# A graph-attention layer and a mixture-of-experts layer in one kernel: three reorderings, at the start and at the join of the two layers

## The chip, the cores and the metric

The kernel runs on one core of a Trainium2 chip. The metric is the device time of one execution in microseconds (us). A core has a tensor engine (PE in the profile, its weight loads PEld), a vector engine (DVE), a scalar engine (ACT), GpSimd (POOL) and a sync engine (SP) that here only issues DMAs. Each engine runs its own list of instructions in order and waits on semaphores for the others.

## The reference, cut to what matters

```python
x = x + gnn(layernorm(x), adj, W, a1, a2)      # x: 1354 x 512, adj: 1354 x 1354
#   h = input @ W; f1 = h @ a1; f2 = h @ a2
#   e = leaky_relu(f1 + f2.T, 0.2); attention = softmax(where(adj > 0, e, -9e15), axis=1)
#   gnn = relu(attention @ h)
x = x + ffn(layernorm(x))                       # 8 experts, 512 -> 512 -> 512
#   logits = x @ Wr + br; each token goes to its one best expert, with its softmax weight as gate
#   pos = rank of the token within its expert; tokens with pos >= 1354 // 8 = 169 are dropped
#   expert input = gate * x; hidden = relu(in @ W1 + b1); out = gate * (hidden @ W2 + b2)
```

Everything is float32. Ranks start at 1, so an expert takes up to 168 tokens (CAP).

## The kernel before, in words

Tokens lie in 11 tiles (NT) of 128 rows; the last, tile 10, has 74. There is no planner: the order of each engine's work is written out by hand, as calls one after the other, and semaphores say what each waits for.

**The start.** SP and ACT issue the loads: half of tile 0 of x each, then W in four chunks on ACT's queue, and on SP's queue a1, tile 1 of x, a2, and, once the first chunk of W is there, tiles 2 to 10 and adj. PE first runs five matmuls on constants (spin). Then it spreads a1 over the partitions (spread_a(0), L1373), turns tile 0 (x_turn(0), L1390: four transposes), spreads a2, and multiplies tile 0 by the left half of W (h_raw(0, 0), L1403). Tile 1 follows: x_turn(1), h_raw(1, 0), x_turn(2), then the right halves h_raw(0, 1) and h_raw(1, 1), which need W @ a1 and W @ a2 as two more columns. Those columns come from DVE's dots (L863), four instructions for each of a1 and a2, which need what spread_a left in a bank. The layer norm of a tile is split: DVE takes bn_stats and bn_aggr (stats, L811 and L816), POOL makes rstd and shift (power, L397 to L402), and ACT applies them (normal, L509); tile 0 alone is normalised by DVE (L825). ACT also copies the turned tile out of its bank (x_high, L518) and rounds the parts of W (w_high, L550). From tile 2 on the products are split in high and low parts (h_product, L1421). All the f2 sums meet in f2_turn (L1449).

**Attention.** For each tile scores, softmax, transposes of the probabilities (p_turn, L1469) and their product with h (attend, L1488; attend_last, L1502, for tile 10, in two halves of 256 columns).

**The join.** Tiles 0 to 7 are routed early: the rows of expert 0 among them are gathered by row number (gather_early) into x1_g[0], as 128 rows (j = 0) and 40 rows (j = 1). prepare_first on DVE normalises them and multiplies by the gate into xg0 (L1135); turn_first on PE transposes xg0 (L1609) into the banks of gx0_ps, the input of expert 0. c = 2 and 3 of it use a bank that holds tile 10's attention output until ACT has read it (s_rl 2). Rows of tiles 8 to 10 that go to expert 0 are added there by late_first (L1621), a matmul of the normalised tile with a matrix place_e0 that holds the gate at the row's place (places_first, L1085; place_last, L1096). Tile 10 takes this way: relu_last on ACT (L667, two halves), residual_last on DVE (L971), stats2 (L977), variance2, POOL's power2 (L433) and shift (L454), normal_last on ACT (L674); and beside it x2_turn on PE (L1514), x2_copy on ACT (L658), logits on PE (L1525), then biased, choose, gates and place_last on DVE. first_layer_first (L1740) is expert 0's first product. The rows of the other experts are gathered by POOL (L458) once all rows of x1 are stored. Experts 1 to 7 follow, bound to PE's order.

The names and lines that the change touches: load_x in SP's list, x_high(1) and w_high(1) in ACT's, dots and stats(1) in DVE's; and at the join prepare_first, residual_last, gates (split in zsums and inverses), ranks(1), turn_first with the spins around x2_turn(NT - 1, 0), and the wait of normal_last.

Of the kernel before, what the change touches and what calls it, by code (L numbers as in the profile page):

```python
# [37 lines left out]
def gat_moe(nc, x, adj, W, a1, a2, Wr, br, W1, b1, W2, b2, out):  # L38
# [29 lines left out]
    with ExitStack() as ctx:  # L68
# [208 lines left out]
        def _(sp):  # L277
            def load_x(t):
                R = rows(t)
                w = D if t else H0  # L280
                sp.dma_start(x_all[0:R, t, 0:w], x[t * P:t * P + R, 0:w]).then_inc(s_x[t], 16)

            load_x(0)
            for a, i in ((a1, 0), (a2, 1)):
                sp.wait_ge(s_zero, i + 1)
                sp.dma_start(a_rows[0:1, i, :], a.rearrange("n o -> o n")).then_inc(s_a[i], 16)
                if i == 0:
                    load_x(1)
            sp.wait_ge(s_w[0], 16)
# [207 lines left out]
        def _(act):  # L497
# [74 lines left out]
            w_high(0)  # L572
            normal(1)
            w_high(1)
            x_high(1)
            normal(2)
# [83 lines left out]
            def relu_last():  # L660
# [4 lines left out]
                for j, (done, n) in enumerate(((s_o, NT), (s_ohi, 1))):  # L665
                    act.wait_ge(done, n)
                    act.activation(relu_s[0:R, j * H0:(j + 1) * H0], o_ps[j][0:R, 0:H0], ACT.Relu,  # L667
                                   scale=rinv[0:R, (NT - 1) % 2, :]).then_inc(s_rl, 1)

            def normal_last():  # L670

                R = rows(NT - 1)
                act.wait_ge(s_sh2, 1)
                act.activation(xn2[NT - 1 - EARLY][0:R, :], x_all[0:R, NT - 1, 0:D], ACT.Identity,  # L674
                               scale=x_all[0:R, NT - 1, D + 1:D + 2], bias=shift[0:R, NT - 1:NT]).then_inc(s_xn2, 1)
# [50 lines left out]
            exp_below(1)  # L726
            relu_last()
            x2_copy(NT - 1, 0)
            normal_last()
# [77 lines left out]
        def _(dve):  # L807
# [69 lines left out]
            normal_first()  # L877
            dots(0, 0, 2)
            stats(1)
            dots(0, 2, KC)  # L880
            stats(2)
# [83 lines left out]

            def residual_last():
                t, R = NT - 1, rows(NT - 1)
                for j in range(2):
                    c = slice(j * H0, (j + 1) * H0)
                    dve.wait_ge(s_rl, j + 1)  # L970
                    ins = dve.tensor_tensor(x_all[0:R, t, c], x_all[0:R, t, c], relu_s[0:R, c], ALU.add)  # L971
                ins.then_inc(s_x1, 1)

# [55 lines left out]

            def gates(b):  # L1030


                t0, t1 = BATCH[b]
                dve.wait_ge(s_expl, b + 1)
                dve.tensor_reduce(zsum[:, t0:t1], expl[:, t0:t1, :], AX.X, ALU.add).then_inc(s_zsum, 1)
                dve.wait_ge(s_zsum, b + 1)
                dve.reciprocal(gate[:, t0:t1], zsum[:, t0:t1]).then_inc(s_gate, 1)
# [88 lines left out]
            def prepare_first():  # L1126


                dve.wait_ge(s_x1g[0], 32)
                dve.wait_ge(s_gate0, 1)  # L1130
                dve.tensor_tensor(scale_s[:, 0, :], x1_g[0][:, :, D + 1], gate0[:, :],
                                  ALU.mult).then_inc(s_scale, 1)
                dve.wait_ge(s_scale, 1)
                for j in range(2):
                    dve.tensor_scalar(xg0[0:S[j], j, :], x1_g[0][0:S[j], j, 0:D], x1_g[0][0:S[j], j, D:D + 1],  # L1135
                                      scale_s[0:S[j], 0, j:j + 1], ALU.subtract, ALU.mult).then_inc(s_xg, 1)

# [33 lines left out]
            for t in range(1, NT - 1):  # L1171
# [22 lines left out]
                if t == 2:  # L1194
                    biased(0)
            gates(0)
            token_and_gate(0)
# [11 lines left out]
            prepare_first()  # L1209
            residual_last()  # L1210
            stats2(NT - 1, 0)
            variance2(NT - 1, 0)
            gates(1)
            ranks(1)
            places_first(1, NT - 3)
            places_first(1, NT - 2)
            biased(NT - 1)
            choose(2)
            gates(2)
            place_last()  # L1220
# [75 lines left out]
            def final_first():  # L1296


                dve.wait_ge(s_x1g[0], 64)
                for j in range(2):  # L1300
                    dve.wait_ge(s_y, j + 1)
                    dve.wait_ge(s_xg, j + 1)
                    v = x1_g[0][0:S[j], j, 0:D]
                    dve.scalar_tensor_tensor(v, y_ps[j][0:S[j], :], gate_s[0:S[j], j, 0:1], v, ALU.mult, ALU.add
                                             ).then_inc(s_fin, 1)
# [51 lines left out]
        def _(pe):  # L1357
# [241 lines left out]

            def turn_first(c0, c1):  # L1600


                pe.wait_ge(s_xg, 2)
                for j in range(2):
                    for c in range(c0, c1):
                        if j == 0 and c == 2:
                            pe.wait_ge(s_rl, 2)
                        o = (c % 2) * CAP
                        pe.matmul(gx0_ps[c // 2][:, o + j * P:o + j * P + S[j]],  # L1609
                                  xg0[0:S[j], j, c * P:(c + 1) * P], ident[0:S[j], 0:S[j]],  # L1610
                                  start=(c % 2 == 0 and j == 0), stop=False, is_transpose=True)

# [89 lines left out]
            positions(2, True)  # L1702
            turn_first(0, KC)
            spin(2, slots_ps)
            x2_turn(NT - 1, 0)
            spin(2, slots_ps)
            logits(NT - 1, 0)
# [168 lines left out]
```

## Time and profile before

| | us |
|---|---|
| median of 3 runs | 259.79 |
| the runs | 258.88, 259.79, 261.66 |
| profiled execution, its own time | 260.57 |
| its span | 258.8 |
| PE busy | 247.0 (95%) |
| DVE busy | 188.4 (73%) |
| ACT busy | 133.8 (52%) |
| POOL busy | 88.7 (34%) |

The span runs from the first to the last instruction of the profiled execution; 1.77 us of its own time lie around it. PE is busy nearly throughout, so time can only be saved where PE waits or is slow.

### The profile page before, as it was taken

How to read it: one execution, taken by the hardware profiler on the slowest of the kernel's cores; microseconds unless marked ns; L12 is line 12 of the kernel's file. 1: busy time of each engine (PE TensorE's matmuls, PEld its weight loads, DVE VectorE, ACT ScalarE, POOL GpSimd, SP SyncE). 2: the span in 40 equal slices, each digit the busy share in tenths (PEclk: the TensorE clock that was granted, in tenths of full speed). 3: DMA queues.
4: the chain of work that ended last, by engine and by line, in shares of the span. 5: the costliest groups of instructions: out<-in, count | busy, mean ns of one | idle time of the engine just before them, and what ended most of it. 6: DMA issues, size and time to landing. Idle time of an engine off the chain costs nothing.

```text
span 258.8 us, 4589 instructions
## 1 busy us (share of the span) xinstructions
PE 247.0 (95%) x1625; PEld 208.9 (81%) x1625; DVE 188.4 (73%) x451; ACT 133.8 (52%) x289; POOL 88.7 (34%) x114
## 2 busy tenths in 40 slices
PE   6799999999999899999999999999999999999990
PEld 1489999988788687787787889899978879879780
DVE  3967849997899989888973563866476974974941
ACT  2735785884756765766672320342365364463330
POOL 4324783000024413441330224108462355321522
PEclk9979999999999999999999999999999999999997
DMA  6991000023347779841212204044988798887101
GB/s 223 354 305 42 1 4 1 7 103 107 107 150 174 250 298 276 232 153 62 81 41 84 82 0 137 12 155 131 344 296 264 247 324 294 267 297 248 49 7 44
DMA packets 19210, 40.47 MB, mean 156 GB/s; under 512 B 2810, under 2 KB 3130, under 8 KB 19188
## 3 DMA queue, kind: packets, MB, share of 16 engines
q1 hardware_dynamic: 16196, 34.17, 40.6%
q0 software_dynamic: 2176, 4.80, 5.5%
q10 hardware_dynamic: 816, 1.21, 1.3%
q8 instruction: 13, 0.21, 0.4%
q14 instruction: 9, 0.07, 0.1%
HBM read 32.93 MB, written 8.31 MB: 159 GB/s over the span
## 4 chain that ended last, share of the span: by engine, by line
PE 77%; DVE 9%; ACT 4%; issue 4%; POOL 3%; DMA 1%; POOLq 1%; ACTq 0%
PE bank L1488 21%; PE bank L1754 12%; PE bank L1792 7%; PE bank L1421 6%; PE bank L1820 5%; PE bank L1469 4%; PE bank L1502 3%; PE bank L1403 3%; PE bank L1740 2%; PE bank L1767 2%; DVE adj_s L918 2%; PE bank L1514 1%; PE bank L1621 1%; DVE adj_s L940 1%; PE bank L1525 1%
## 5 line engine op out<-in xcount | busy, mean ns | idle before, releaser
L1488 PE MATMUL bank<-h_hi,pt_hi 128*128 128x512 f32 (+1 forms) x110 | 43.2, 393 | 0.0
L1488 PE MATMUL bank<-h_hi,pt_lo 128*128 128x512 f32 x100 | 41.8, 418 | 0.0
L1488 PE MATMUL bank<-h_lo,pt_hi 128*128 128x512 f32 x100 | 39.1, 391 | 0.0
L428 POOL TENSOR_TENSOR x_all<-x_all,w_raw 128x512 f32<-128x512 f32 x10 | 21.3, 2127 | 50.4 <-ACT w_raw L617 46.7
L1754 PE MATMUL bank<-prob,w 128*128 128x168 f32 x224 | 33.2, 306 | 0.1
L1754 PEld LDWEIGHTS bank<-prob,w 128*128 128x128 f32 x224 | 32.6, 189 | 0.9 <-issue 0.3
L789 ACT ACTIVATE adj_s<-bank,b_cols 128x168 f32<-128x168 f32 x28 | 11.2, 402 | 33.3 <-PE bank L1754 33.3
L1488 PEld LDWEIGHTS bank<-h_hi,pt_hi 128*128 128x128 f32 (+1 forms) x110 | 20.6, 188 | 4.7
L640 ACT ACTIVATE wide<-adj_s,off_b 128x1354 f32<-128x1354 f32 (+1 forms) x11 | 15.7, 1430 | 12.3 <-DVE off_b L933 12.2
L1488 PEld LDWEIGHTS bank<-h_lo,pt_hi 128*128 128x128 f32 x100 | 18.9, 189 | 3.1
L1488 PEld LDWEIGHTS bank<-h_hi,pt_lo 128*128 128x128 f32 x100 | 18.8, 188 | 3.0
L433 POOL TENSOR_TENSOR x_all<-ve,half 128x1 f32<-128x1 f32 (+1 forms) x11 | 6.1, 553 | 42.5 <-DVE ve L984 42.5
L465 POOL DMA_INDIRECT out_dram<-x_all,first x10 | 12.1, 1208 | 23.6 <-DVE x_all L1325 16.6
L940 DVE SCALAR_TENSOR_TENSOR adj_s<-adj_s,off_a,wide 128x1354 f32<-128x1354 f32 (+1 forms) x11 | 17.9, 1629 | 1.3 <-ACT wide L640 1.0
L955 DVE TENSOR_TENSOR pt_lo<-bank,pt_hi 128x512 fp32r<-128x512 f32 (+1 forms) x22 | 14.6, 666 | 5.1 <-ACT pt_hi L628 4.7
L1278 DVE TENSOR_TENSOR h_lo<-adj_s,h_hi 128x256 fp32r<-128x256 f32 x14 | 5.9, 424 | 16.9 <-ACT h_hi L790 16.8
L1469 PE MATMUL bank<-ident,prob 128*128 128x128 f32 (+3 forms) x121 | 18.0, 274 | 0.0
L628 ACT ACTIVATE pt_hi<-bank 128x512 fp32r<-128x512 f32 (+1 forms) x22 | 12.6, 579 | 10.4 <-PE bank L1469 10.4
L918 DVE CUSTOM_DVE_ANT_0 adj_s<-adj_s,wide 128x1354 f32<-128x1354 f32 (+1 forms) x11 | 17.2, 1568 | 0.8 <-ACT wide L569 0.6
L1269 DVE TENSOR_TENSOR h_lo<-w,h_hi 128x1024 fp32r<-128x1024 f32 x14 | 16.5, 1220 | 0.1
L458 POOL DMA_INDIRECT x_all<-x_rows,first x10 | 9.9, 991 | 16.5 <-PE bank L1724 8.5
L1469 PEld LDWEIGHTS bank<-ident,prob 128*128 128x128 f32 (+3 forms) x121 | 13.8, 146 | 1.9 <-issue 1.0
(227 smaller groups left out, 578.7 us busy)
## 6 DMA issues: line engine op xcount, KB each, us to landing
w<-in_L_ffn_W_dram SPq DMA_DIRECT2D x16, 1024.0 KB, 6.8
adj_s<-in_adj_dram SPq DMA_DIRECT2D x10, 677.0 KB, 5.7
x_rows<-x_all SPq DMA_DIRECT2D x10, 257.0 KB, 3.6
out_dram<-x_all SPq DMA_DIRECT2D x10, 256.0 KB
x_all<-in_x_dram SPq DMA_DIRECT2D x9, 256.0 KB, 5.6
prob<-in_L_ffn_b_dram SPq DMA_DIRECT2D x5, 256.0 KB, 7.2
w_raw<-in_L_gnn_W_dram ACTq DMA_DIRECT2D x4, 256.0 KB, 5.4
adj_s<-in_L_ffn_b_dram SPq DMA_DIRECT2D x2, 256.0 KB, 7.2
```

Of the source, the lines that this page charges most:

```text
L428: pool.tensor_tensor(x_all[0:R, t, 0:D], x_all[0:R, t, 0:D], relu_s[0:R, :], ALU.add).then_inc(s_x1, 1)
L640: act.activation(score2[0:R, :], arg[t % 3][0:R, :], ACT.Identity, scale=SLOPE, bias=off_b[0:R, t % 2, :]).then_inc(s_low, 1)
L918: dve.tensor_tensor_reduce(arg[t % 3][0:R, :], arg[t % 3][0:R, :], f2b[0:R, :], 1.0, LEAST, ALU.add, ALU.max, fmax[0:R, t % 2, :]).then_in ...
L940: dve.scalar_tensor_tensor(arg[t % 3][0:R, :], arg[t % 3][0:R, :], off_a[0:R, t % 2, :], score2[0:R, :], ALU.add, ALU.max).then_inc(s_arg, 1)
L955: dve.tensor_tensor(pt_lo[:, par, k0:k1, 0:R], v[:, :, 0:R], pt_hi[:, par, k0:k1, 0:R].bitcast(F32), ALU.subtract).then_inc(s_plo[b], 1)
L1269: dve.tensor_tensor(w2_lo[par][:, c, :], w2_s[:, par, c, :], w2_hi[par][:, c, :].bitcast(F32), ALU.subtract).then_inc(s_w2lo, 1)
L1421: ins = pe.matmul(h_ps[par][j][0:R, 0:c1 - c0], a[:, par, c, 0:R], w[:, c, c0:c1], start=(n == 0 and c == 0), stop=(n == 2 and c == KC - 1))
L1469: ins = pe.transpose((pt_ps if t else pt0_ps)[b][0:K, o:o + R], prob[0:R, par, k * P:k * P + K], ident[0:R, 0:R])
L1488: ins = pe.matmul(o_ps[par][0:R, :], p[0:K, par, k, 0:R], h[0:K, k, :], start=(k == 0 and n == 0), stop=(k == NT - 1 and n == 1))
L1754: ins = pe.matmul(hid_ps[f // 2][:, (f % 2) * CAP:(f % 2 + 1) * CAP], w1_s[:, par, c, f * P:(f + 1) * P], gx_t[par][:, c, :], start=(c == ...
L1792: ins = pe.matmul(ya_ps[par][:, :], v[par][:, c, :], w[par][:, c, :], start=(c == 0 and n == 0), stop=(c == KC - 1 and n == 2))
L1820: ins = pe.matmul(yb_ps[par][64 * i:64 * i + S[1], 0:H0], hid[par][:, c, P:CAP], w2_s[:, par, c, i * H0:(i + 1) * H0], start=(c == 0), sto ...
```

## The change

On SP, the load of tile 1 of x is issued ahead of a1 and a2; before it stood between them. On DVE, the statistics of tile 1 run ahead of all four dots of a1; before they stood between the second and the third. On ACT, x_high(1) runs ahead of w_high(1).

At the join, the 40 late rows of the first gathered set (j = 1) are normalised and scaled by ACT (gathered_last, by scale and bias) and no longer by DVE; DVE only makes their shift, one instruction on a column. turn_first is called once for each j: the 128 rows ahead of x2_turn of tile 10, the 40 rows behind it. Of the four spins around x2_turn one is left. The two halves of residual_last have ranks(1) between them. gates(1) is split: the sum of exponentials runs ahead of the scaling, the reciprocal ahead of residual_last. normal_last waits for s_sh2 at 2, as gathered_last has its first count.

```diff
             load_x(0)
+            load_x(1)
             for a, i in ((a1, 0), (a2, 1)):
                 sp.wait_ge(s_zero, i + 1)
                 sp.dma_start(a_rows[0:1, i, :], a.rearrange("n o -> o n")).then_inc(s_a[i], 16)
-                if i == 0:
-                    load_x(1)
...
             normal(1)
+            x_high(1)
             w_high(1)
-            x_high(1)
...
+            def gathered_last():
+
+                act.wait_ge(s_sh2, 1)
+                act.activation(xg0[0:S[1], 1, :], x1_g[0][0:S[1], 1, 0:D], ACT.Identity, scale=scale_s[0:S[1], 0, 1:2],
+                               bias=shift[0:S[1], 0:1]).then_inc(s_xg, 1)
...
             relu_last()
+            gathered_last()
             x2_copy(NT - 1, 0)
             normal_last()
...
             normal_first()
-            dots(0, 0, 2)
             stats(1)
-            dots(0, 2, KC)
+            dots(0)
             stats(2)
...
+                zsums(1)
                 dve.wait_ge(s_scale, 1)
-                for j in range(2):
-                    dve.tensor_scalar(xg0[0:S[j], j, :], x1_g[0][0:S[j], j, 0:D], x1_g[0][0:S[j], j, D:D + 1],
-                                      scale_s[0:S[j], 0, j:j + 1], ALU.subtract, ALU.mult).then_inc(s_xg, 1)
+                dve.tensor_scalar(xg0[:, 0, :], x1_g[0][:, 0, 0:D], x1_g[0][:, 0, D:D + 1], scale_s[:, 0, 0:1],
+                                  ALU.subtract, ALU.mult).then_inc(s_xg, 1)
+                dve.tensor_scalar(shift[0:S[1], 0:1], x1_g[0][0:S[1], 1, D:D + 1], -1.0, scale_s[0:S[1], 0, 1:2],
+                                  ALU.mult, ALU.mult).then_inc(s_sh2, 1)
+                inverses(1)
...
             prepare_first()
-            residual_last()
+            residual_last(0)
+            ranks(1)
+            residual_last(1)
             stats2(NT - 1, 0)
             variance2(NT - 1, 0)
-            gates(1)
-            ranks(1)
             places_first(1, NT - 3)
...
             positions(2, True)
-            turn_first(0, KC)
-            spin(2, slots_ps)
+            turn_first(0)
+            spin(1, slots_ps)
             x2_turn(NT - 1, 0)
-            spin(2, slots_ps)
+            turn_first(1)
             logits(NT - 1, 0)
```

## Rows read from the trace of the kernel before

**Rows 1.** Chain of waits: start us, length us, what; the start, then f2_turn.

```profile
9.60 0.28 POOL shift L402
...
12.25 3.26 PE bank L1403 x8
15.51 0.85 PE bank L1390 x4
...
40.15 2.65 PE bank L1449 x22
```

**Rows 2.** Timeline of PE, start: start us, length, line, operation, [idle before <-releaser].

```profile
3.97 2.05 PE L1373 MATMUL bank<-vecs,half 128*128 128x512 f32 x2 [0.29 <-DMA vecs<-in_L_gnn_a_dram]
...
7.87 1.98 PE L1403 MATMUL bank<-w_raw,x2t 128*128 128x256 f32 x8
10.82 0.66 PE L1390 MATMUL bank<-ident,w 128*128 128x128 f32 x4 [0.97 <-ACT w L509]
```

**Rows 3.** Timeline of DVE, start.

```profile
5.91 0.55 DVE L825 TENSOR_SCALAR w<-x_all,mv,rstd 128x512 f32<-128x512 f32 x1 [1.12 <-POOL rstd L399]
...
7.61 0.69 DVE L811 BATCH_NORM_STATS2 stat<-x_all 128x6 f32<-128x512 f32 x1
```

**Rows 4.** Timeline of ACT, start.

```profile
8.55 1.06 ACT L550 ACTIVATE w_hi<-w_raw 128x1024 fp32r<-128x1024 f32 x1 [0.74 <-DMA w_raw<-in_L_gnn_W_dram]
...
11.63 0.57 ACT L518 ACTIVATE x2t<-bank 128x512 f32<-128x512 f32 x1
```

**Rows 5.** Stretches: length, busy us by engine, granted clock (1.00 is full), DMA.

```profile
12.50:13.00 0.50, 0.50 (x3) 0.45 (x3) 0.50 (x3) 0.40 (x1) 0.00 (x0) 0.83 1.15 302
...
16.00:16.50 0.50, 0.50 (x4) 0.47 (x3) 0.18 (x2) 0.10 (x1) 0.42 (x2) 0.76 0.98 260
...
84.50:88.00 3.50, 2.50 (x15) 1.74 (x16) 2.94 (x10) 3.40 (x7) 0.75 (x2) 1.00 0.78 313
```

**Rows 6.** DMA queues, 4 to 6.5 us: SP's queue q1, packets, MB, share.

```profile
q1 hardware_dynamic: 141, 0.26, 31.7%
```

**Rows 7.** Chain of waits at the join.

```profile
164.26 1.02 PE bank L1609 x8
165.28 0.54 PE bank L1364 x2
165.82 0.27 PE bank L1514 x4
...
169.10 1.94 PE bank L1621 x12
```

**Rows 8.** Timeline of PE from 164.6 us: the 40-row transposes.

```profile
164.84 0.44 PE L1609 MATMUL bank<-ident,adj_s 40*128 40x40 f32 x4
```

**Rows 9.** Timeline of DVE at the join.

```profile
163.21 0.99 DVE L1135 TENSOR_SCALAR adj_s<-wide,scale_s 128x512 f32<-128x512 f32 x2
164.13 0.74 DVE L971 TENSOR_TENSOR x_all<-x_all,w_raw 74x256 f32<-74x256 f32 x2
164.91 0.69 DVE L977 BATCH_NORM_STATS2 stat<-x_all 74x6 f32<-74x512 f32 x1
...
166.49 0.64 DVE L1085 TENSOR_SCALAR wide<-place,first,gate 128x168 f32<-128x168 f32 x2
...
169.15 0.37 DVE L1096 TENSOR_SCALAR wide<-place,bank,gate 128x168 f32<-128x168 f32 x1
```

**Rows 10.** Timeline of ACT at the join.

```profile
163.79 0.47 ACT L667 ACTIVATE w_raw<-bank,rinv 74x256 f32<-74x256 f32 x1 [0.39 <-PE bank L1502]
166.12 0.42 ACT L658 ACTIVATE x2t<-bank 128x296 f32<-128x296 f32 x1 [1.86 <-PE bank L1514]
167.21 0.81 ACT L674 ACTIVATE adj_s<-x_all,shift 74x512 f32<-74x512 f32 x1 [0.68 <-POOL shift L454]
```

**Rows 11.** Timeline of POOL: the first late gather.

```profile
174.51 1.09 POOL L458 DMA_INDIRECT wide<-x_rows,first  x1 [7.33 <-DMA x_rows<-x_all]
```

**Rows 12.** Timeline of DVE: prepare(1) for expert 1.

```profile
179.06 0.15 DVE L1236 TENSOR_TENSOR scale_s<-wide,first 128x1 f32<-128x1 f32 x1
```

More of the change, by code:

```diff
@@ L668, in relu_last @@
                                    scale=rinv[0:R, (NT - 1) % 2, :]).then_inc(s_rl, 1)
+            def gathered_last():
+                act.wait_ge(s_sh2, 1)
+                act.activation(xg0[0:S[1], 1, :], x1_g[0][0:S[1], 1, 0:D], ACT.Identity, scale=scale_s[0:S[1], 0, 1:2],
+                               bias=shift[0:S[1], 0:1]).then_inc(s_xg, 1)
             def normal_last():
                 R = rows(NT - 1)
-                act.wait_ge(s_sh2, 1)
+                act.wait_ge(s_sh2, 2)
                 act.activation(xn2[NT - 1 - EARLY][0:R, :], x_all[0:R, NT - 1, 0:D], ACT.Identity,
@@ L964, in p_low, with residual_last @@
                                       ).then_inc(s_plo[b], 1)
-            def residual_last():
+            def residual_last(j):
                 t, R = NT - 1, rows(NT - 1)
-                for j in range(2):
[L969 to L972, printed above, removed]
+                c = slice(j * H0, (j + 1) * H0)
+                dve.wait_ge(s_rl, j + 1)
+                ins = dve.tensor_tensor(x_all[0:R, t, c], x_all[0:R, t, c], relu_s[0:R, c], ALU.add)
+                if j:
+                    ins.then_inc(s_x1, 1)
             def stats2(t, par):
@@ L1028, in choose, with zsums @@
                                   ).then_inc(s_onehot, 1)
-            def gates(b):
+            def zsums(b):
                 t0, t1 = BATCH[b]
@@ L1035, in gates, with inverses @@
                 dve.tensor_reduce(zsum[:, t0:t1], expl[:, t0:t1, :], AX.X, ALU.add).then_inc(s_zsum, 1)
+            def inverses(b):
+                t0, t1 = BATCH[b]
                 dve.wait_ge(s_zsum, b + 1)
@@ L1132, in prepare_first @@
                                   ALU.mult).then_inc(s_scale, 1)
+                zsums(1)
                 dve.wait_ge(s_scale, 1)
-                for j in range(2):
-                    dve.tensor_scalar(xg0[0:S[j], j, :], x1_g[0][0:S[j], j, 0:D], x1_g[0][0:S[j], j, D:D + 1],
-                                      scale_s[0:S[j], 0, j:j + 1], ALU.subtract, ALU.mult).then_inc(s_xg, 1)
+                dve.tensor_scalar(xg0[:, 0, :], x1_g[0][:, 0, 0:D], x1_g[0][:, 0, D:D + 1], scale_s[:, 0, 0:1],
[3 more added lines that the diff above has]
+                inverses(1)
             penalty(0)
@@ L1195, in _ @@
                     biased(0)
-            gates(0)
+            zsums(0)
+            inverses(0)
             token_and_gate(0)
@@ L1218, in _ @@
             choose(2)
-            gates(2)
+            zsums(2)
+            inverses(2)
             place_last()
@@ L1301, in final_first @@
                     dve.wait_ge(s_y, j + 1)
-                    dve.wait_ge(s_xg, j + 1)
+                    dve.wait_ge(s_xg, 2)
                     v = x1_g[0][0:S[j], j, 0:D]
@@ L1598, in wr_mean, with turn_first @@
                 ins.then_inc(s_wrm, 1)
[L1600 to L1611, printed above, removed]
+            def turn_first(j):
+                pe.wait_ge(s_xg, j + 1)
+                for c in range(KC):
+                    if j == 0 and c == 2:
+                        pe.wait_ge(s_rl, 2)
+                    o = (c % 2) * CAP
+                    pe.matmul(gx0_ps[c // 2][:, o + j * P:o + j * P + S[j]],
+                              xg0[0:S[j], j, c * P:(c + 1) * P], ident[0:S[j], 0:S[j]],
+                              start=(c % 2 == 0 and j == 0), stop=False, is_transpose=True)
             def late_first(t, c0, c1):
```

## The prediction

> **What bounds the kernel now.** I read the chain of waits first, for where time on PE can be saved at all, then the timelines of PE, DVE and ACT in the two stretches that the diff touches, then the granted clock there. The chain is PE for most of the span. In the first stretch it runs over the statistics of tile 1, POOL's shift (done 9.88) and ACT to h_raw(1, 0), which starts at 12.25 [rows 1]. PE waits 0.97 us ahead of x_turn(1) [rows 2], and again between its end (10.82 + 0.66 = 11.48) and 12.25, 0.77 us. Then the reader should look at durations: h_raw(1, 0) takes 3.26 us [rows 1], the same eight records for tile 0 took 1.98 [rows 2]. The stretches say why: the granted clock goes from 1.00 to 0.50 (2.4 to 1.2 GHz) inside 12.5 to 13 and comes back inside 16 to 16.5 [rows 5]. At the join the chain is PE alone: turn_first 164.26, two spins 165.28, x2_turn 165.82, and the last twelve records of late_first to 171.04 [rows 7]. x2_turn's data were there at 164.13 + 0.74 = 164.87 [rows 9]; it stood behind turn_first and spins for 0.95 us. That is the second thing to win.
>
> **The start, part by part.** On DVE stats(1) can start when normal_first ends, 5.91 + 0.55 = 6.46, in place of 7.61 [rows 3]: 1.15 us earlier. POOL's shift follows by as much, 8.73 in place of 9.88 [rows 1]. ACT doesn't follow so far: w_high(0) holds it until 8.55 + 1.06 = 9.61 [rows 4], so normal(1) starts about then. It ended just ahead of x_turn(1) at 10.82 before; with 0.81 for such an operation [rows 10] it started at about 9.97. It gains 0.37, and x_turn(1) moves to 10.45. The other 0.78 us of the statistics' lead are covered by w_high(0) and worth nothing. x_high(1) stood behind w_high(1) and started at 11.63 [rows 4]; it can now start when x_turn(1) is done, 10.45 + 0.66 = 11.11. So h_raw(1, 0) moves from 12.25 to 11.72: **0.53 us**, of which 0.37 are the statistics and 0.16 the order on ACT.
>
> What is pushed back: w_high(1) now ends at about 11.65 + 1.06 = 12.7, and normal(2), behind it, at about 13.5. x_turn(2) wants that when h_raw(1, 0) is over: 11.72 + 1.98 = 13.7 at full clock, later at the low one. Covered, by 0.2 us in the tighter case. The dots of a1 keep their number and only swap places with stats(1), so the last dot ends as before. From h_raw(1, 0) on PE runs without a wait of note, and what comes later on DVE, POOL and ACT waits for PE's results; I take the 0.53 as carried to f2_turn at 40.15 [rows 1] and on to the end, between 0 (something late that I don't see) and 0.53.
>
> The queue that this is moved past: a1 is 2 KB and now stands behind tile 1's 256 KB on SP's queue. Before, a1 had landed by 3.97, when spread_a(0) started [rows 2], and tile 1's 0.26 MB went through SP's queue between 4 and 6.5 us, beside ACT's load of W [rows 6]. Issued some 0.65 us earlier they would be through at 5.6 or so (an estimate from those rows), and a1 lands between 4.0 (if it isn't held) and 5.9. The wait of 0.29 us ahead of spread_a(0) grows by as much as 1.9. spread_a(0) took 2.05 us, which at 3.97 is twice what the same work takes later, so it ran at the low clock. Started at 5.6 it ends between 6.7 and 7.6; x_turn(0), which could start at 6.46, starts up to 1.0 later. PE has 0.97 - 0.37 = 0.60 us of idle left ahead of x_turn(1) to take that. Loss between 0 and 0.4; I take 0.1, as a1 must be very late to cost more. DVE's dots start behind stats(1), at about 7.3, and want spread_a(0) by then: nothing or 0.3, under the slack that the dots have until h_raw(0, 1).
>
> The Trainium skill, page "DMA: Bandwidth & Descriptors", section "Queues, rings and completion order", says that each DMA engine takes the descriptors of one ring in their order, and shares itself between rings. By it a1 can't land ahead of its engine's share of tile 1. Before, a1 stood ahead of tile 1 and landed ahead of it, so the trace agrees but doesn't test it. It makes the late end of the bounds above the nearer one, and is the rule that speaks against this change; the third rival below is what it would give.
>
> **The join, part by part.** PE's stream: turn_first for the 128 rows is 164.84 - 164.26 = 0.58 us [rows 7, 8]; c = 2 of it waits for relu_last, done at 163.79 + 0.47 = 164.26 [rows 10], before it is reached. One spin is 0.27 [rows 7]. So x2_turn can start at 164.26 + 0.58 + 0.27 = 165.11. Its data: DVE makes one scaling of 0.5 where it made two (0.99 for both), plus a shift on a column, a sum and a reciprocal, each 0.1 to 0.2 in such a row of single columns (I take 0.1 of pitch), then the halves of residual_last around ranks(1). The second half waits for 164.26 in any case, and ends at about 164.7 in place of 164.87 [rows 9]. So PE is the limit: **0.71 us** earlier for x2_turn. The 40 rows' transposes, 0.4 us [rows 8], now lie behind it, in the time in which ACT copies the turned tile (0.42) [rows 10], where two spins lay; they wait for gathered_last. That is on ACT behind relu_last: 164.26 + 0.81 = 165.07, against 165.4 when x2_turn is over. It fits, and x2_copy isn't held either. If gathered_last took more than 1.1 us, the difference would be lost one for one.
>
> So logits end 0.71 earlier, at 166.57. late_first then wants places_first, 166.49 to 167.13 before [rows 9]: the tile's statistics come 0.19 earlier, and sum, reciprocal and ranks no longer stand between, so about 0.6 in all, the first at 166.2. Covered. Last comes place_last, 169.15 + 0.37 = 169.52 before [rows 9]. Its chain starts from the logits (0.71 earlier), but the exponential of the last batch stands behind normal_last on ACT, and that follows POOL's shift, which is only 0.19 earlier: normal_last 167.02 to 167.83, the exponential to 168.0. The sum that waits for it was at 168.46 and can be at 168.05, 0.41 earlier. PE gets to the last late_first at about 169.0 and may wait up to 0.15. Gain at the join: between 0.41 and 0.71, I take **0.6**.
>
> Behind the join: the late gathers wait for the store of tile 10's rows, not for PE [rows 11], and that store moves by only 0.19. prepare(1) runs at 179.06 with no wait ahead [rows 12]; it may lose some of its lead, and the experts' chain stays on PE. I cost it at nothing, and at 0.4 if that lead is gone.
>
> **The clock.** Of 260.57 us, the low stretch costs 3.26 - 1.98 = 1.28 in h_raw(1, 0) and half of x_turn(2)'s 0.85, 1.7 us together [rows 1, 2]. Ahead of it PE had idled 0.97 and 0.77 us; now these are 0.60 and 0.61 or so. Between 84.5 and 88, with 1.0 us idle, the clock stayed at 1.00 [rows 5]. So it may stay here too; nothing in the trace decides it. At the join three spins go, but their place is taken by real work or cut out, and PE idles no more than 0.2 us at a time; I cost that at nothing.
>
> The sum: 0.53 - 0.1 + 0.6 = 1.0 us with the low stretch still there. The profiled execution took 260.57 (span 258.8 and 1.77 around), so it would take 259.5; it lies 0.78 above the median of 259.79. On the median, 258.8. I lower it by 0.2 for runs in which the clock holds: **258.6**.
>
> **The rivals.** (1) The low clock stretch goes or shrinks, as PE idles less: 0.53 + 1.7 + 0.6, so 257.0. For it: the rows at 84.5; against: the idle left is only 0.5 us less. (2) The join gives nothing, as the exponential or ACT's extra 0.81 takes it back: 259.3. (3) a1 is late by the full 1.9 and the start gives nothing: 259.2, PE's second wait being longer. (4) Slower: the longer idle ahead of spread_a(0) keeps PE at 1.2 GHz until after h_raw(0, 0), and the stretch at 12.8 comes all the same. h_raw(0, 0) then takes 3.26 for 1.98, and x_turn(0) and spread_a(1) some 0.8 more; 2.1 less the 0.60 of slack and 0.5 of the order's gain is +1.0, less 0.6 at the join: 260.2. It decides if a1 lands after 5 us or so and the low clock outlasts 8 us. (5) The change does nothing measurable in either place: 259.8.
>
> **How the numbers follow.** Forecast 0.42; (1) 0.24; (2) 0.08; (3) 0.12; (4) 0.09; (5) 0.05. The range takes in (1) to (4) and leaves out their tails: 256.8 to 260.4. One per cent is 2.6 us, about what a measurement of this kernel can tell from no change. Only (1), at 257.0 with 257.2 as the bound, is faster by more, and about half of it: 0.17. Slower by over 1% would take two of the losses together: 0.04. Within: 0.79.
>
> **What would show it.** h_raw(1, 0) starting at 11.7; normal(1) right behind w_high(0); x2_turn of tile 10 at 165.1 less what the start gave, and the last late_first ending 0.6 earlier than the start alone explains. Wrong if spread_a(0) starts after 5 us and x_turn(0) after 7, if the granted clock is low at other places, or if PE waits for place_last by more than 0.3.

## The result, and the profile after

The changed kernel took 261.43 us (median of 21 runs, 259.89 to 264.96), the kernel before 259.79 (21 runs, 258.88 to 262.89). The ratio is 1.0047, 95% interval 1.0026 to 1.0068: slower by half a per cent, within 1% of no change, and outside the range of 256.8 to 260.4. The profiled execution of the changed kernel is its slowest, 264.96 us with a span of 263.2, one of four that the ratio leaves out as slow; how much of its loss the others have, the experiments show.

Three points split its span, with those of the kernel before beside them. Tile 2's product starts at 20.80 (before 20.93), first_layer_first at 170.46 (171.10), the end is at 263.2 (258.8). So the start gained 0.13, the stretch with the join 0.51, and behind it 92.7 us stand for 87.7: 5.0 us lost in this execution, where the prediction had put nothing.

**The start.** The timeline of PE, then of DVE, then of ACT (start, us, engine, line, operation, tiles, shapes, count, idle before it and what ended that):

```profile
5.62 2.05 PE L1386 MATMUL bank<-vecs,half 128*128 128x512 f32 x2 [1.93 <-DMA vecs<-in_L_gnn_a_dram]
7.46 1.06 PE L1403 MATMUL bank<-ident,w 128*128 128x128 f32 x4
8.31 1.92 PE L1386 MATMUL bank<-vecs,half 128*128 128x512 f32 x2
10.02 2.66 PE L1416 MATMUL bank<-w_raw,x2t 128*128 128x256 f32 x8
12.52 0.60 PE L1403 MATMUL bank<-ident,w 128*128 128x128 f32 x4
13.80 2.00 PE L1416 MATMUL bank<-w_raw,x2t 128*128 128x256 f32 x8 [0.69 <-ACT x2t L517]
```

```profile
6.00 0.69 DVE L817 BATCH_NORM_STATS2 stat<-x_all 128x6 f32<-128x512 f32 x1
```

```profile
9.05 1.05 ACT L549 ACTIVATE w_hi<-w_raw 128x1024 fp32r<-128x1024 f32 x1
10.00 0.80 ACT L508 ACTIVATE w<-x_all,shift,rstd 128x512 f32<-128x512 f32 x1
```

DVE and ACT do what was planned: tile 1's statistics at 6.00 for 7.61 [rows 3], its normal form at 10.00, right behind w_high(0). But a1 ends PE's wait only at 5.62, for 3.97 before [rows 2]. So h_raw(0, 0) comes 2.15 us later (10.02 for 7.87). PE and no longer ACT sets x_turn(1), which starts at 12.52 where the prediction had 10.45, and h_raw(1, 0) starts at 13.80, not 11.7. What pays this back is the clock. Windows of the same execution (busy us of PE, PEld, DVE, ACT, POOL, then the granted clock, DMA share, GB/s):

```profile
12.50:13.00 0.50, 0.50 (x5) 0.36 (x3) 0.50 (x3) 0.00 (x0) 0.00 (x0) 1.00 1.70 321
16.00:16.50 0.50, 0.50 (x5) 0.46 (x3) 0.50 (x2) 0.23 (x1) 0.50 (x1) 1.00 0.93 260
185.50:189.00 3.50, 3.37 (x12) 3.40 (x13) 1.20 (x4) 0.00 (x0) 0.92 (x1) 0.52 1.01 339
```

The low stretch of 12.8 to 16.2 [rows 5] isn't there, and h_raw(1, 0) takes 2.00 us for 3.26 [rows 1]. PE came up from the low clock later, at 11.57 us for 6.00 (its product of tile 0 is still slow, 2.66 for 1.98), and then kept the high one. These two times are the starts of the first records of the granted clock in the traces. Ahead of them the windows print 1.00 all the same, and the low clock shows in PE's durations alone: spread_a(0) takes 2.05 us, the same work in spread_a(1) of the kernel before 1.02.

**The join.** Timeline of PE there:

```profile
163.94 0.64 PE L1621 MATMUL bank<-ident,adj_s 128*128 128x128 f32 x4
...
164.63 0.44 PE L1527 MATMUL bank<-ident,x_all 74*128 74x74 f32 x4
165.00 0.44 PE L1621 MATMUL bank<-ident,adj_s 40*128 40x40 f32 x4
...
169.02 1.38 PE L1633 MATMUL bank<-wide,adj_s 74*128 74x168 f32 x8 [0.17 <-DVE wide L1104]
170.46 1.38 PE L1752 MATMUL bank<-prob,w 128*128 128x168 f32 x8
```

As planned: the 128 rows, one spin, x2_turn at 164.63, the 40 rows behind it. In the same timeline of the kernel before x2_turn starts at 165.66 (the chain of [rows 7] counts it from 165.82, where the spin ahead of it ends), so it is 1.03 earlier, of which the start gave 0.13. The last late_first now waits 0.17 us for place_last on DVE.

**Behind the join.** Rows of ACT, POOL and DVE around expert 1's turn, a fence for each timeline:

```profile
184.69 0.60 ACT L750 ACTIVATE prob<-bank 128x512 f32<-128x512 f32 x1 [5.72 <-remote]
```

```profile
185.43 0.99 POOL L457 DMA_INDIRECT x_all<-x_rows,first  x1 [2.18 <-remote]
```

```profile
181.81 0.69 DVE L1305 TENSOR_SCALAR adj_s<-bank,b_cols 128x168 f32<-128x168 f32 x2 [2.02 <-PE bank L1779]
```

PE's side of the same stretch:

```profile
180.80 0.52 PE L1736 MATMUL bank<-ident,w_raw 104*128 104x104 f32 x4
181.16 0.60 PE L1791 MATMUL bank<-ident,adj_s 128*128 128x128 f32 x4
182.55 0.66 PE L1791 MATMUL bank<-ident,adj_s 128*128 128x128 f32 x4 [0.80 <-DVE adj_s L1305]
185.63 6.49 PE L1766 MATMUL bank<-prob,w 128*128 128x168 f32 x32 [2.42 <-ACT prob L753]
```

And the same copy of ACT in the kernel before:

```profile
182.00 0.60 ACT L744 ACTIVATE prob<-bank 128x512 f32<-128x512 f32 x1 [2.38 <-PE bank L1724]
```

ACT's copy of expert 1's turned rows waits for one semaphore that PE's last transpose (L1736) increments, and POOL's gather of expert 3's rows waits for the same increment. The last transpose starts at 181.07 and should take 0.25; in the kernel before, the copy began 0.29 us behind the start of that transpose. Here it begins 3.62 behind, and POOL 0.74 behind ACT, as it does (0.74 or 0.75) in the six other traces in which both wait. Two engines on one semaphore, both late by the same time, with nothing of their own in the way: PE's increment itself is seen late. The trace's records of semaphore events say the same. Of the 153 increments that can be paired with matmuls, the median comes 0.29 us behind the matmul's start; this one comes 3.60 behind, and the neighbours on PE 1.56 (DVE's wait of 2.02 above), 2.03 and 1.85. In the trace of the kernel before, none behind the first 12 us comes later than 0.44. DVE's own increment beside them (L1305) comes 0.01 us behind its instruction's end. PE then idles 2.42 us, its granted clock falls to 0.50 when it goes on, and expert 1's first product takes 6.49 us where one at full clock takes 4.82 (join_second).

The Trainium skill, page "Perfetto Trace Analysis", section "Per-engine timelines", says that TensorE's increment goes out when PSUM has acknowledged the last write, and that the profile's end of a matmul is estimated from its size. By it the rows above can't tell a late write from a late message; no run here does either.

### The profile page after: what moved, and what is told of

Read it like the earlier page. It is cut to its first block, busy times and chain, and to the rows that moved or that the text cites. A ratio compares the mean times of both kernels' runs of the same rounds, so it can differ in the third digit from the quotient of the medians.

```text
span 263.2 us, 4583 instructions
## 1 busy us (share of the span) xinstructions
PE 247.9 (94%) x1622; PEld 210.6 (80%) x1622; DVE 188.1 (71%) x451; ACT 134.4 (51%) x290; POOL 88.0 (33%) x114
## 4 chain that ended last, share of the span: by engine, by line
PE 74%; DVE 10%; issue 4%; ACT 4%; POOL 3%; another core or an unknown queue 2%; DMA 1%; POOLq 1%; ACTq 0%; DVEq 0%
PE bank L1501 21%; PE bank L1766 13%; PE bank L1804 7%; PE bank L1434 6%; PE bank L1832 5%; PE bank L1482 4%; PE bank L1416 3%; PE bank L1515 2%; PE bank L1752 2%; DVE adj_s L923 2%; DMA vecs<-in_L_gnn_a_dram 1%; PE bank L1386 1%; PE bank L1527 1%; DVE adj_s L945 1%
## 5 line engine op out<-in xcount | busy, mean ns | idle before, releaser
L1766 PE MATMUL bank<-prob,w 128*128 128x168 f32 x224 | 34.9, 315 | 2.4 <-ACT prob L753 2.4
L1766 PEld LDWEIGHTS bank<-prob,w 128*128 128x128 f32 x224 | 34.2, 198 | 3.2 <-issue 2.7
```

What stands on the lines that cost most here:

```text
L1766: ins = pe.matmul(hid_ps[f // 2][:, (f % 2) * CAP:(f % 2 + 1) * CAP], w1_s[:, par, c, f * P:(f + 1) * P], gx_t[par][:, c, :], start=(c == ...
```

## The experiments

Each column of times is from the one profiled execution of that kernel; ratio, median and count are of its timed runs against the kernel before on the same chip. "Tile 2" is the start of its product, "FLF" of first_layer_first, "rest" from there to the end, "ACT idle" the wait ahead of the copy of expert 1's rows, "over" the runs of 261.5 us or more. M is the first measurement; the other letters are five chips. Each was measured in one session, so that a chip and its time can't be told apart.

| kernel | chip | ratio (95%) | median | over | tile 2 | FLF | rest | ACT idle |
|---|---|---|---|---|---|---|---|---|
| before | M | 1 | 259.79 | 4/21 | 20.93 | 171.10 | 87.7 | 2.38 |
| changed | M | 1.0047 (1.0026-1.0068) | 261.43 | 9/21 | 20.80 | 170.46 | 92.7 | 5.72 |
| join_only | A | 0.9986 (0.9956-1.0015) | 259.10 | 1/12 | 19.48 | 169.15 | 87.8 | 2.38 |
| start_only | A | 0.9990 (0.9966-1.0014) | 259.54 | 0/12 | 18.66 | 168.86 | 87.7 | 2.38 |
| load_only | A | 1.0003 (0.9983-1.0023) | 259.79 | 0/12 | 20.05 | 170.25 | 88.4 | 2.38 |
| a1_back | A | 0.9959 (0.9928-0.9991) | 258.96 | 0/12 | 20.71 | 170.42 | 87.8 | 2.38 |
| after_again | B | 0.9952 (0.9929-0.9975) | 258.88 | 0/12 | 19.43 | 169.07 | 88.0 | 2.38 |
| a12_first | B | 0.9967 (0.9943-0.9990) | 258.97 | 0/12 | 20.27 | 169.96 | 87.7 | 2.38 |
| a1_pool | B | 1.0031 (1.0001-1.0062) | 260.98 | 2/12 | 19.96 | 170.30 | 87.9 | 2.38 |
| after_spin | B | 0.9899 (0.9866-0.9932) | 257.74 | 0/6 | 18.46 | 168.13 | 87.9 | 2.38 |
| after_third | C | 1.0037 (1.0010-1.0064) | 260.93 | 3/12 | 19.78 | 169.45 | 92.4 | 5.42 |
| before_spin | C | 1.0039 (1.0003-1.0076) | 260.65 | 5/12 | 23.09 | 173.26 | 87.7 | 2.38 |
| a1_back_spin | C | 1.0030 (0.9993-1.0067) | 260.73 | 4/12 | 19.08 | 168.69 | 89.5 | 4.13 |
| a1_act | C | 1.0021 (0.9982-1.0060) | 259.85 | 3/12 | 18.52 | 168.17 | 89.4 | 4.08 |
| after_fourth | D | 1.0069 (1.0043-1.0094) | 261.26 | 5/12 | 18.93 | 168.62 | 89.4 | 4.07 |
| join_second | D | 1.0079 (1.0048-1.0110) | 262.03 | 7/12 | 19.91 | 169.61 | 89.5 | 4.17 |
| start_second | D | 0.9993 (0.9969-1.0017) | 259.40 | 0/12 | 19.87 | 170.05 | 87.8 | 2.38 |
| small_w | D | 1.0139 (1.0085-1.0192) | 263.17 | 5/6 | 19.24 | 168.96 | 91.7 | 4.86 |
| join_late | E | 0.9994 (0.9962-1.0025) | 258.84 | 0/12 | 19.32 | 169.42 | 87.7 | 2.38 |
| gathers_late | E | 0.9986 (0.9954-1.0018) | 259.02 | 0/12 | 19.16 | 169.31 | 87.7 | 2.38 |

The kernel before had 3 of 35 such runs on A, 3 of 29 on B, 6 of 35 on C, 4 of 29 on D, 2 of 23 on E. "Over" isn't the mark of the late increment: before_spin has 5 such runs, and in its profile ACT's wait is 2.38.

### The halves: join_only, start_only, load_only, a1_back

join_only is the diff's part at the join alone. start_only is its part at the start, as in the diff, with the join as before; load_only has of that the SP part alone:

```diff
             load_x(0)
+            load_x(1)
             for a, i in ((a1, 0), (a2, 1)):
                 ...
-                if i == 0:
-                    load_x(1)
```

a1_back is the changed kernel with these lines as they were before.

> The join's edits alone, the start as before. Theory 1 (a1 lands late behind tile 1's load, the start loses, the join gains): 0.5 to 0.7 us faster than before; PE's first 20 us as before, spread_a(0) at about 4.0. Theory 2 (the join's edits cost later what they gain, at the gathers and expert 1): no gain or up to 1 us slower. Last record of late_first 0.6 us earlier than before by both.

> All three edits of the start, the join as before. Theory 1: spread_a(0) at about 5.6, h_raw(1, 0) at 13 to 14 in place of 12.25, 1 to 2 us slower than before. Theory 2: within 0.4 us of before, as the later a1 is taken up by PE's idle time.

> The kernel before with one edit: tile 1's load is issued ahead of a1 and a2. The orders on DVE and ACT are as before, so the first two dots hold stats(1) back. Theory 1: spread_a(0) at about 5.6, dots from 7.7, stats(1) at about 9 in place of 7.6, and 1.5 to 2.5 us slower, the worst of these four. Theory 2: no difference over 0.4 us.

> The changed kernel with one edit undone: a1 is issued ahead of tile 1's load again. Theory 1: spread_a(0) at about 4.0, h_raw(1, 0) at 11.7 as the prediction had it, 1.1 us faster than before, and up to 2.8 if the low clock stretch after 12.8 goes too; the best of these four. Theory 2: as slow as the changed kernel, 1 us or so slower than before.

From tile 2's product to FLF it is 150.2 us in the kernels without the join's part (before 150.17, start_only 150.20, load_only 150.20) and 149.7 in those with it (join_only 149.67, a1_back 149.71, changed 149.66). **The join gives 0.5 us**, in these profiles and in all later ones but two: join_late, whose three spins take it back, and a1_pool, where f2_turn waits 1.02 us for 0.37 and 150.3 are left. The start is harder to read, since the clock moves it: join_only, whose start is that of the kernel before, reaches tile 2 at 19.48, 1.45 us sooner; its clock rose only at 10.0 us and didn't fall again. In load_only spread_a(0) starts at 5.10 for 3.97, and nothing is gained for it; the loss of 1.5 to 2.5 us that was expected of it by theory 1 isn't there either. In a1_back, where a1 is ahead again, tile 1 lands too late for its statistics:

```profile
7.46 0.69 DVE L818 BATCH_NORM_STATS2 stat<-x_all 128x6 f32<-128x512 f32 x1 [1.39 <-DMA x_all<-in_x_dram]
```

They start 0.15 us sooner than in the kernel before, and h_raw(1, 0) at 12.03. So the order on DVE needs the order on SP. a1_back is the fastest of the four, by 0.4% or 1.1 us, which is what theory 1 expected, though not by the h_raw(1, 0) at 11.7 that was to bring it. None of the four is slower here, and the changed kernel's two halves can't be what the first measurement showed, if this chip is like that one.

### Again, and a1's place: after_again, a12_first, a1_pool, after_spin

after_again is the changed kernel. a12_first has tile 1 behind both a1 and a2 on SP's queue; a1_pool lets POOL issue a1; after_spin has nine spins for five ahead of spread_a(0).

```diff
-            spin(5)
+            spin(9)
```

> The changed kernel, unchanged, beside the others on one chip. The start's edits alone came out even with before (0.999) and the join's alone 0.14% faster, so by a sum of the parts it is 0.2 to 0.3% faster than before here. If the two sets of edits hurt each other (theory 2 in a new form: with both, something after the join is late), it is again 0.3 to 0.7% slower, and its profile shows a wait behind 170 us that the others lack.

> The changed kernel with both a1 and a2 ahead of tile 1's load, so that the load is issued 0.3 us later than before. Theory of the late a1: like a1_back, 0.3 to 0.6% faster than before; spread_a(0) at about 3.8. If tile 1's own landing is what counts, stats(1) waits at 6 us and the time is that of before or worse.

> The changed kernel with tile 1's load still first on SP's queue, but a1 sent over POOL's queue. If a1 is late since it stands behind tile 1 in one ring, it now lands by about 4 and the time is that of a1_back, 0.3 to 0.6% faster than before. If it is late since the DMA engines are full, it lands at 5 to 5.6 here too, and the time stays that of the changed kernel.

> The changed kernel with nine constant matmuls at PE's start in place of five, 1.7 us more of them at the low clock, to fill the wait for a1. If the cost of the late a1 is that PE's clock comes up later, h_raw(0, 0) runs at full clock here and the time is 0.5 to 1.5 us below that of the changed kernel. If the cost is the wait alone, the time stays.

On this chip the changed kernel is **faster**, 0.9952, its 12 runs between 258.35 and 259.68. a12_first puts PE's first wait back (spread_a(0) at 4.00) and is no better; its statistics of tile 1 wait for the load until 8.06. a1_pool says nothing on the ring: POOL issued its DMA by 2.48, but of the 32 packets of its queue 2 moved between 4.5 and 5.0 and 30 between 5.0 and 5.5. after_spin is the fastest kernel of this study where it ran. PE's timeline there:

```profile
1.36 4.02 PE L1377 MATMUL bank<-ones 128*128 128x512 bf16 x9 [1.36 <-POOL ones L367]
5.18 1.17 PE L1386 MATMUL bank<-vecs,half 128*128 128x512 f32 x2
...
7.75 1.98 PE L1416 MATMUL bank<-w_raw,x2t 128*128 128x256 f32 x8
```

The spins fill the wait for a1, spread_a(0) runs mostly at full clock (1.17 for 2.05; the first clock record starts at 5.37), and h_raw(0, 0) is at 7.75 and 1.98 long, although spread_a(0) starts no sooner than in after_again (5.15), where h_raw(0, 0) is at 9.42.

### A third chip: after_third, before_spin, a1_back_spin, a1_act

before_spin and a1_back_spin are those kernels with nine spins. a1_act is the changed kernel with a1 issued on ACT's queue ahead of W, and no longer on SP's:

```diff
+            act.wait_ge(s_zero, 1)
+            act.dma_start(a_rows[0:1, 0, :], a1.rearrange("n o -> o n")).then_inc(s_a[0], 16)
```

> The changed kernel once more, unchanged. So far the ratio to the kernel before was 1.0047 and, on another chip, 0.9952. If the ratio belongs to the chip or its state at the time, it comes out anywhere between these and the profile's first 20 us tell how late a1 was and where the clock came up: each 0.1 us of PE's start of tile 2's product (20.9 in the kernel before) is 0.1 us of time. If the first measurement was the kernel's own, it is 1.004 or more again.

> The kernel before with nine constant matmuls at PE's start in place of five. They end at about 5.4, past a1's landing at 4.0, so spread_a(0) starts 1.4 us late. If the clock at the start is what counts, this still gains: the clock is up by 6 in every run and doesn't fall at 12.8, tile 2's product starts at 19 to 19.5, 1 to 1.5 us faster than before. If only a1's landing and the order of the work count, it is as before or up to 1 us slower.

> The changed kernel with a1 ahead of tile 1's load and nine constant matmuls. The changed kernel with nine of them took 257.7, 1.0% below before. If a1's place in the queue costs nothing once the wait for it is filled, this is the same, 257.5 to 258. If it still costs, this is 0.5 us or more below.

> The changed kernel with tile 1's load first on SP's queue and a1 sent on ACT's queue, ahead of the chunks of W (which start 0.5 us later for it). Over POOL's queue a1 landed at 6.1, but that queue's own packets came only at 5 to 5.5, so it told nothing of the ring. If a1 is late since it stands behind tile 1 in SP's ring, it lands at about 4 here. If the engines are full, at 5 or later. The time is 0 to 0.6% below before in the first case, less what W's delay costs.

PE's timeline of a1_act:

```profile
4.10 1.71 PE L1387 MATMUL bank<-vecs,half 128*128 128x512 f32 x2 [0.42 <-DMA vecs<-in_L_gnn_a_dram]
...
10.18 0.66 PE L1404 MATMUL bank<-ident,w 128*128 128x128 f32 x4 [0.40 <-ACT w L509]
11.52 2.00 PE L1417 MATMUL bank<-w_raw,x2t 128*128 128x256 f32 x8 [0.69 <-ACT x2t L518]
```

Tile 1 is still first on SP's queue and the DMA engines as full (a share of about 1 from 2.5 us on, as in after_third), yet spread_a(0) starts 0.9 us sooner than in the changed kernel on the same chip (4.99), and 1.5 sooner than on M. So a1's lateness is its place behind tile 1 in one queue. Without it x_turn(1) and h_raw(1, 0) come at 10.18 and 11.52, near where the prediction put them (10.45, 11.72); here the clock also rose early, at 5.35. Windows of before_spin show that spins don't make the clock safe; it rose at 5.1 and fell for 7 us:

```profile
11.75:18.75 7.00, 6.26 (x18) 4.92 (x19) 5.38 (x13) 2.96 (x5) 2.88 (x6) 0.51 1.02 302
```

The gain that was expected of before_spin isn't there (1.0039). And on this chip the late increment is back: after_third, a1_back_spin and a1_act all have ACT's long wait, before_spin has not. Their "rest" is 4.7, 1.8 and 1.7 us longer than before's 87.7; the largest is that in which the clock fell behind it.

### Which half brings it: after_fourth, join_second, start_second, small_w

The changed kernel, join_only and start_only once more; and the changed kernel with less of the weights:

```diff
-                sp.dma_start(w1_s[:, e % 2, :, :], W1[e, :, :]...
+                k = D if e < 2 else 64
+                sp.dma_start(w1_s[:, e % 2, :, 0:k], W1[e, :, 0:k]...
```

(w2 likewise.)

> The changed kernel once more, on another chip. If the stall ahead of expert 1's first product belongs to the change (theory A), about half of its executions lie at 261.5 us or more and its ratio is 1.003 to 1.005; if it belongs to the chip or to chance (theory B), this depends on the chip: where no execution has it, the time is 258.9 and the ratio 0.995 as in the second job. In the profile, either the stretch from first_layer_first to the end is 87.7 to 88.0 us (no stall) or 92 to 93 us (stall).

> The change at the join alone. Theory A1, that the join's half gm brings the stall, since it puts PE 0.5 us further ahead of the late gathers: a share of its executions at 261.5 or more like that of after_fourth, ratio about 1.003. Theory A2, that the start's half brings it: none of its executions there, ratio about 0.998. Product of tile 2 to first_layer_first again 149.7 us against 150.2 in the kernel before.

> The change at the start alone. Theory A1 (the join's half brings the stall): none of its executions at 261.5 or more, ratio 0.999. Theory A2 (the start's half): as after_fourth, ratio about 1.003. Product of tile 2 to first_layer_first 150.2 us, as in the kernel before.

> The changed kernel, with the loads of the weights of experts 2 to 7 cut to 64 of their 512 columns, so that these experts compute with what the buffers held: its output is not the reference's. If the stall comes from the late gathers standing among the packets of expert 2's weights (theory C), none of its executions has it, its slowest execution is within 1.5 us of its fastest, and its time is 258.5 to 259.5. If the stall has nothing to do with that load (theory D), as many of its executions have it as of after_fourth, and the profile of one shows ACT's copy of expert 1's gathered rows released 2 to 3 us behind PE's last transpose all the same.

**The time is lost with the join's half.** Side by side on one chip, join_second is 1.0079 with 7 of 12 runs over 261.5, start_second 0.9993 with none. The fastest runs say it without any threshold: start's half 258.33 us on A and 258.34 on D, join's half 258.63 and 260.17; the changed kernel 258.35 on B, but 259.89, 259.90 and 259.81 on M, C and D. So some 1.5 us are lost there in the fastest runs too, and not only in those "over". ACT's rows, of join_second and then of start_second:

```profile
182.30 0.60 ACT L751 ACTIVATE prob<-bank 128x512 f32<-128x512 f32 x1 [4.17 <-remote]
```

```profile
180.94 0.60 ACT L743 ACTIVATE prob<-bank 128x512 f32<-128x512 f32 x1 [2.38 <-PE bank L1722]
```

But start_second has late increments too, one place further on. ACT's first copy of expert 1's hidden layer, in start_second and then in start_only:

```profile
185.31 0.40 ACT L788 ACTIVATE adj_s<-bank,b_cols 128x168 f32<-128x168 f32 x1 [3.57 <-PE bank L1752]
```

```profile
183.26 0.40 ACT L788 ACTIVATE adj_s<-bank,b_cols 128x168 f32<-128x168 f32 x1 [2.71 <-PE bank L1752]
```

In start_only it begins 2.57 us behind the start of expert 1's first product, as it does in all profiles on A, B and E and in that of the kernel before. In start_second it is 3.43, in before_spin on C 3.41: two kernels without the join's part. In join_second and after_fourth, beside start_second on D, it is 2.57 again, and the increment ahead of it is the late one. The semaphore records agree: PE's increment for it comes 1.18 and 1.16 us behind its matmul, and one at the end of the transposes ahead of the product (L1777 and L1779) 0.82 and 0.81. Nothing waits on the critical path there, so "rest" stays at 87.8 and 87.7. The late increments belong to these measurements, then, and the join's half decides which increment is late, and by how much: with it, it is one for which PE has to wait.

small_w refutes the theory for which it was made: with an eighth of the bytes of those weights the increment is late all the same (4.86), and the kernel the slowest of the four. The weights' volume isn't the cause.

### PE's lead: join_late, gathers_late

In all kernels with the join's part PE stands further ahead of the late gathers: the first is issued 3.8 to 4.1 us behind FLF, 3.3 to 3.5 in the others, since FLF came forward by 0.5, and the gathers, which wait for the store of tile 10's rows, hardly moved. join_late is join_only with three spins and gives the lead back; gathers_late, the kernel before with one instruction on POOL, was to make it without the edit:

```diff
+            spin(3, slots_ps)
             late_first(NT - 1, 2, KC)
```

```diff
             pool.wait_ge(s_src, 1)
+            pool.tensor_tensor(rstd[:, 0:1], rstd[:, 0:1], half[:, :], ALU.pow)
```

> The change at the join, with three matmuls on constants (0.21 us each) ahead of PE's last four matmuls of late_first, so that first_layer_first starts 0.5 to 0.6 us later against the gathers; the first late gather is again issued 3.3 to 3.5 us behind the start of first_layer_first, as in the kernel before (3.40), where the join edits had 3.8 to 4.1. Theory T (PE's lead over the gathers brings the late increments): no execution at 261.5 us or more beyond what the kernel before shows, ratio 1.000 to 1.001, ScalarE's copy of expert 1's rows right behind PE's transposes. Theory E (something else in the edit brings them): as join_second on its chip, ratio 1.003 to 1.009. On a chip that never shows the late increments, both give 1.000 to 1.001.

> The kernel before, with one GpSimd power on a dead column (0.55 us by the row of its kind) ahead of the first late gather, so that all late gathers, the load of expert 2's weights and the scaling of expert 1's rows come 0.5 to 0.6 us later against PE, which is the place that they have in the kernels with the change at the join. Theory T: a third to a half of the executions at 261.5 us or more, ratio 1.003 to 1.008. Theory E: none of them, ratio 0.999 to 1.001, since the gathers of the kernel before have slack (expert 1's rows are scaled by 180.4 us, PE asks for them at 181.1). On a chip that never shows the late increments, both give 0.999 to 1.001.

join_late's first gather is back at 3.44 behind FLF, its profile has no late increment, and none of its 12 runs is over 261.5. That fits the theory of the lead; but it ran on a chip where nothing shows that any kernel would have it. The intended control failed, as POOL's timeline in gathers_late says:

```profile
171.91 0.55 POOL L472 TENSOR_TENSOR rstd<-rstd,half 128x1 f32<-128x1 f32 x1 [6.53 <-DMA x_rows<-x_all]
172.63 1.09 POOL L458 DMA_INDIRECT wide<-x_rows,first  x1 [0.18 <-issue]
```

The gather starts 0.72 us behind the end of the wait with the added instruction; where none is there it starts 0.74 behind the moment at which the same increment released ACT. So the 0.55 us were free, the gathers (3.33 behind FLF) weren't moved, and this run tests neither theory.

## Why the prediction was wrong

**a1's lateness.** "Loss between 0 and 0.4; I take 0.1, as a1 must be very late to cost more": mis-sized, 2.07 us in this execution (x_turn(1) at 12.52 for 10.45). The bounds for the landing held (spread_a(0) at 5.62 in the changed profile, 4.99 to 5.23 in its repeats), but h_raw(0, 0) behind it moved by 2.15 us, against 0.60 of slack. The step had looked at the start of spread_a(0) alone; it left out the clock that PE's next work would meet. In this execution it rose at 11.57 us in place of 6.00, so x_turn(0) took 1.06 for 0.66, spread_a(1) 1.92 for 1.02, h_raw(0, 0) 2.66 for 1.98, together 1.98 us on PE's own path. This is rival (4)'s first half, near its price (2.1). How much of it is a1's doing is not settled: with a1 behind tile 1 and five spins the clock rose at 7.8 to 11.6 us in all eight profiles, but with the old start at 6.0 in one and 5.4, 9.6, 9.8 and 10.0 in others. Of the wait alone, without the clock, 0.95 us reached x_turn(0) (7.46 for 6.51).

**The 0.53 of the start.** Right as a mechanism, but only with tile 1's load first: a1_act, which has the edit without a1's delay, put h_raw(1, 0) at 11.52 for 11.72; a1_back, where the load is behind a1 again, at 12.03. In the changed kernel it wasn't to be had, since PE came late itself.

**The clock.** "So it may stay here too; nothing in the trace decides it" held. In all eight profiled executions with a1 behind tile 1 and five spins the low stretch was gone; wherever the clock rose to 2.4 GHz later than 7 us, with the new start or the old one, it did not fall again in this stretch, and where it rose between 4.4 and 6.1 it fell in three of seven. So rival (1)'s 1.7 us and rival (4)'s loss came together and nearly cancelled: 0.13 gained up to tile 2, for 0.43 forecast. That these are near each other is luck.

**The join.** Right, and the nearer bound was the lower one: 0.5 for 0.6. x2_turn gained more than the 0.71 (0.90 without the start's 0.13), and the last late_first had to wait 0.17 for place_last, whose chain runs over POOL's shift, normal_last and the exponential, as the prediction had it: place_last starts at 168.50 for 169.15, 0.52 earlier once the start's 0.13 is taken off.

**Behind the join: the step that failed.** "I cost it at nothing, and at 0.4 if that lead is gone." The lead of prepare(1) over PE did hold (DVE's rows were done at 179.8, PE asked at 180.4). What came was of another kind: in three of six measurements (M, C and D; M's chip may be one of the others) the increment for ACT's copy of expert 1's rows is seen late, PE waits 1.8 to 3.1 us for that copy, and the experts' chain is 1.7 to 1.8 us longer, or 4.0 to 5.0 where the clock falls to 0.50 behind PE's wait. All seven profiles with the join's part on M, C and D have this; none of the three without it, and none of the seven with it on A, B and E. It turns the 0.64 us gained up to FLF into a loss of 0.47% on M; on B, where it is absent, the same kernel gains 0.48%. No rival had it. The forecast's 258.6 is near what B measured (258.88), in part by luck: the join's term is confirmed there, the start's isn't, since it hangs on when the clock rose.

**What stays open.** That the join's edit costs the time where increments are late is shown, by join_second beside start_second. Why increments are late isn't, nor why the edit moves the delay onto the one for which PE waits; nor whether it is the chip or the time of the measurement that brings them. PE's longer lead over the gathers is argued from join_late and from the rows' order alone; the bytes of the weights are excluded; the edit's other effects (three matmuls fewer, ACT's added instruction) were not tried apart, and join_late, which puts three matmuls back, couldn't tell them from the lead even where the fault is. It was not tried there.

## What to carry to other kernels

A small load put behind a large one on the same queue is late (2 KB behind 256 KB: the work that wants it starts at 4.96 to 5.62 us, for 3.73 to 4.00 here), and TensorE's next work is then moved and may still be at the low clock; another queue (here ACT's) takes most of the wait back. Read the duration of a first product as well as its start. A gain of half a microsecond near a place where two engines hang on one increment of TensorE has to be measured on several chips, and with the parts of the change side by side, before it is believed: this change is 0.5% faster on one and 0.7% slower on another. When an engine's wait ends without a releaser in the profile, look for a second engine on the same semaphore; both late alike points to the sender. And look for the same fault in the kernels that don't lose time by it: here they had it too.

## What the runs showed of the hardware

- TensorE's increments can be seen 1.6 to 4.2 us behind their matmul's start where the median is 0.29, in one stretch of a program and in three of six measurements, with DVE's on time; kernels that differ a little have them at 0.8 and 1.2 us there, at other increments (before_spin, start_second).
- TensorE's clock rises at another time in each execution of the same start (5.4 to 10.0 us in five profiles of the old one), and may fall again; tile 2's product starts between 19.16 and 20.93 in these five.
- A GpSimd indirect DMA starts some 0.74 us behind the end of its wait (seven traces); an instruction of 0.55 us between the two was free (gathers_late).
- A DMA issued by GpSimd early in the kernel (a1_pool) moved nearly all its packets over 2.5 us after the issue, and spread_a(0) started at 6.07; with a1 on SP's queue behind tile 1 it starts at 4.96 to 5.62, on ACT's ahead of W at 4.10, on SP's ahead of tile 1 at 3.73 to 4.00.
